# Deformable convolution and mixture of experts: images in pairs, positions without rows of their own

## The reference, cut to what matters

```python
xl = ln_c(x)                                  # normalised over channels
om = conv3x3(xl, w_off) + b_off               # 27 maps: 9 dy, 9 dx, 9 masks
ys, xs = y + kh - 1 + dy, x + kw - 1 + dx     # sampling places, per tap and pixel
sampled = bilinear(xl, ys, xs) * sigmoid(mask)   # zero outside the image
x = x + einsum('bckhw,ock->bohw', sampled, w_dcn)
t = tokens(x); z = ln_t(t)
w = softmax(top2(z @ Wg + bg))
t = t + sum_e w[e] * (gelu(z @ W1[e] + b1[e]) @ W2[e] + b2[e])
```

## Time and profile before

| | us |
|---|---|
| median of three runs | 90.9 |
| the profiled execution | 90.21 |
| its span, first to last instruction | 88.4 |
| PE busy | 80.9 (92%) |
| DVE busy | 64.5 (73%) |
| ACT busy | 46.9 (53%) |
| POOL busy | 20.6 (23%) |

### The profile page before, as it was taken

One profiled execution on the slowest core, in us unless ns is written; L12 is line 12 of the kernel. 1 busy time (PEld: TensorE's weight loads), 2 busy tenths in 40 slices (PEclk: granted clock), 3 DMA queues, 4 the chain that ended last, 5 costly groups with the idle time before them and its releaser, 6 DMA issues.

```text
span 88.4 us, 1853 instructions
## 1 busy us (share of the span) xinstructions
PE 80.9 (92%) x606; PEld 48.7 (55%) x606; DVE 64.5 (73%) x199; ACT 46.9 (53%) x95; POOL 20.6 (23%) x39
## 2 busy tenths in 40 slices
PE   3986799999999999969969999999999999999970
PEld 3974455499657968846646535734345332433540
DVE  5999989998999999999954998519667613213470
ACT  4110565787956843211410899814439986889000
POOL 7499820000003040005000002200309103200720
DMA  1520049340999997089999500000000000000012
GB/s 32 160 61 2 2 77 399 129 124 15 293 259 319 296 314 259 1 222 272 311 320 320 164 4 0 7 0 0 0 0 0 0 0 0 0 7 0 0 59 59
DMA packets 7192, 9.92 MB, mean 112 GB/s; under 512 B 1690, under 2 KB 3648, under 8 KB 7184
## 3 DMA queue, kind: packets, MB, share of 16 engines
q1 hardware_dynamic: 6848, 9.42, 35.9%
q0 software_dynamic: 192, 0.30, 1.0%
q10 hardware_dynamic: 144, 0.10, 0.3%
HBM read 8.95 MB, written 0.85 MB: 111 GB/s over the span
## 4 chain that ended last, share of the span: by engine, by line
PE 56%; DVE 19%; DMA 11%; issue 5%; SPq 3%; ACT 1%; POOL 1%; DVEq 0%
PE banks L937 17%; PE banks L948 15%; DMA hat_rows<-hlast 6%; DMA spread_hats<-hat_rows 6%; PE banks L861 5%; DVE front L589 4%; PE banks L875 4%; PE banks L830 3%; DVE xn L699 2%; PE banks L848 2%; SPq L335 2%; PE banks L928 1%; PE banks L886 1%; DVE spread_hats L600 1%; PE banks L919 1%
## 5 line engine op out<-in xcount | busy, mean ns | idle before, releaser
L511 ACT ACTIVATE front<-banks,b_col 128x512 f32<-128x512 f32 x32 | 19.8, 700 | 8.7 <-PE banks L937 5.4
L937 PE MATMUL banks<-x2s,w_sb 64*128 64x512 f32 x64 | 15.2, 608 | 0.0
L948 PE MATMUL banks<-front,w_sb 128*64 128x512 f32 (+1 forms) x72 | 14.7, 549 | 0.0
L770 DVE SCALAR_TENSOR_TENSOR spread_hats<-banks,b_col,spread 128x512 f32<-128x512 f32 (+1 forms) x9 | 6.1, 689 | 9.9 <-PE banks L948 7.3
L349 POOL TENSOR_TENSOR rs<-ve,power 128x2 f32<-128x2 f32 (+1 forms) x6 | 5.2, 868 | 28.7 <-DVE ve L639 27.5
L589 DVE TENSOR_TENSOR front<-hats 128x512 f32<-128x512 f32 (+1 forms) x20 | 11.5, 630 | 0.5 <-PE banks L861 0.3
L600 DVE TENSOR_TENSOR spread_hats<-spread_hats 128x1024 f32<-128x1024 f32 (+1 forms) x10 | 10.8, 1107 | 0.7 <-DMA spread_hats<-hat_rows 0.6
L483 ACT ACTIVATE smp<-banks 128x256 f32<-128x256 f32 x14 | 5.2, 389 | 9.5 <-PE banks L875 9.5
L875 PE MATMUL banks<-spread_hats,xn 128*64 128x256 f32 x72 | 9.0, 384 | 0.7 <-DVE spread_hats L600 0.7
L937 PEld LDWEIGHTS banks<-x2s,w_sb 64*128 64x128 f32 x64 | 5.7, 186 | 6.4 <-issue 2.5
L948 PEld LDWEIGHTS banks<-front,w_sb 128*64 128x64 f32 x72 | 4.9, 137 | 7.8 <-issue 6.2
(11 more groups left out here) (117 smaller groups left out, 102.0 us busy)
## 6 DMA issues: line engine op xcount, KB each, us to landing
spread_hats<-hat_rows SPq DMA_DIRECT2D x24, 256.0 KB, 5.0
w_sb<-in_w SPq DMA_DIRECT2D x2, 512.0 KB, 4.6
spread_hats<-hat_rows SPq DMA_DIRECT2D x6, 128.0 KB, 5.6
xc<-in_x_ch SPq DMA_DIRECT2D x1, 256.0 KB, 5.5
hat_rows<-hrow SPq DMA_DIRECT2D x2, 128.0 KB
hat_rows<-hrow POOLq DMA_DIRECT2D x2, 128.0 KB, 5.5
xt<-in_x_tok SPq DMA_DIRECT2D x1, 192.0 KB, 2.5
wdcn<-in_w_dcn SPq DMA_DIRECT2D x1, 160.0 KB, 2.9
```

Source lines behind the costliest of these rows:

```text
L511: act.activation(hid[:, m % H_RING, half, c, :], two_banks(f"H{h}.{j}.{c}")[:, half * 512:(half + 1) * 512], ACT.Gelu, bias=b1_col[:, col: ...
L770: dve.scalar_tensor_tensor(part(tmp[:, h, j, :]), part(bank(step_o)[:, :]), b2_col[:, j:j + 1], part(spread[:, h, j, :]), ALU.add, ALU.mul ...
L937: last = pe.matmul(two_banks(step)[:, half * 512:(half + 1) * 512], w1_sb[rows_, j, c * P:(c + 1) * P], x2s[rows_, 2 * h:2 * h + 2, :], st ...
L948: last = pe.matmul(part(bank(step)[O * half:O * half + O, :]), w2_sb[:, j + PAIRS * half, c, :], part(hid[:, (PAIRS * h + j) % H_RING, hal ...
```

## The change

- Convolution: xnT, xpl, xpu and conv take two images each. The 12 products of a pair go into four groups of 32 rows, two for each image, so that an image has two partial sums in place of four. Statistics are of four tiles and four tiles. xpu of the second pair is ACT's.
- Offsets: one om, one omT, one pos and one tanhm serve both DIRECT images, and one om serves both SPREAD images. The om of the DIRECT pair only copies; that of the SPREAD pair adds bias and pixel positions (pos_rows, made by POOL in place0) while copying, and is DVE's.
- Picking: R1.0 takes y and x of both images with 64 rows each, R1.1 the masks, R1.2 the ninth taps of both. The tap's own shift is the bias of ACT's abs (shift, made by POOL in shift0). The seven DMAs are gone.
- pick is made by two comparisons and two compare-and-add passes on DVE after four POOL iotas, ahead of the frames and the statistics.
- relu0 and relu1 go to ACT, the hat rows are split into y and x, xs1 and xs3 go to DVE, sel0 goes behind rstdt1.
- SP writes the hat rows of both SPREAD images before it issues the first read of them; before, POOL wrote those of image 3.
- All orders and banks are new.

```diff
+IMG_ROWS = 2 * OMG
+POS_ROW = OMG + OM
 PE_ORDER = (
-    "xnT0 early4 conv0 xnT2 xnT3 omT0 xnT1 conv2 conv3 conv1 R2.0 R2.1 R3.1 T0.0 T0.2 T0.3 R3.0 T0.1 T0.4 omT1 T0.5 T0.8 T0.7 "
-    "T0.6 M0.0 M0.4 M0.1 M0.3 M0.2 T1.0 T1.1 T1.3 T1.5 T1.2 T1.4 T1.7 T1.6 T1.8 M1.0 M1.3 M1.2 M1.4 M1.1 C0.0 C1.0 C0.1 C1.1 M2.2 "
-    "oT1 oT0 M2.0 M2.3 M2.1 M2.4 xT0 xT1 C2.0 M3.0 M3.1 C2.1 gate0 H0.2.0 H0.0.0 H0.1.1 H0.1.0 H0.0.1 H0.2.1 oT2 M3.3 M3.2 wdT0 "
...
+    "xnT0 early4 conv0 xnT1 omT0 conv1 R1.0 R1.2 R1.1 T0.5 T0.4 T0.2 T0.3 T0.0 T0.1 M0.2 M0.1 T0.8 M0.0 M0.4 T1.1 T1.0 T0.6 T0.7 "
+    "M1.0 M0.3 T1.3 T1.2 T1.4 T1.6 T1.5 T1.7 T1.8 C0.0 M1.2 M1.1 C0.1 M1.3 M1.4 oT0 C1.0 C1.1 M2.1 M2.0 oT1 M2.3 M2.2 xT0 M2.4 "
+    "C2.0 xT1 C2.1 M3.0 H0.2.0 gate0 H0.0.0 H0.2.1 oT2 H0.0.1 H0.1.1 H0.1.0 M3.1 M3.2 M3.3 O0.0 M3.4 C3.0 O0.2 C3.1 wdT0 xT2 "
...
 ACT_ORDER = (
-    "xpl0 om0 xpl2 xpl3 xpl1 tanhm0 abs0 om2 selr0 om3 ay2 al2 tm2 tl2 om1 E0.0 tm3 E0.3 ay3 E0.1 E0.2 tanhm1 E0.5 abs1 E0.7 E0.6 "
...
+    "xpl0 om0 xpu1 xpl1 tanhm0 abs0 relu0 abs1 relu1 ax2 tl2 al1 tm2 ay2 tl3 E0.5 E0.4 E0.2 E0.3 ay3 tm3 ax3 E0.1 E0.0 E0.8 se0.2 "
...
 DVE_ORDER = (
-    "stats0 stats1 xn0 base0 xpu0 xn2 xn3 xn1 xpu2 xpu3 pos0 dist0 xpu1 relu0 haty0 pr0.1.0 pr0.0.0 pr0.0.1 pr0.1.1 hr2.0 hr2.1 "
-    "hr2.2 pr0.2.0 pr0.2.1 pr0.4.0 pr0.4.1 pr0.3.0 pr0.3.1 pos1 dist1 E0.8 relu1 haty1 pr1.2.1 pr1.0.0 pr1.0.1 pr1.1.0 hr3.0 "
...
+    "stats0 stats1 xn0 xn1 xn2 xpu0 xn3 base0 pos0 dist0 dist1 om1 haty0 pr0.2.1 pr0.2.0 pr0.1.1 pr0.1.0 pr0.0.1 pr0.0.0 hy2 hx2 "
+    "hm2 hl1 pr0.4.1 pr0.4.0 hy3 hx3 haty1 hm3 pr1.0.0 pr1.0.1 pr0.3.1 pr0.3.0 pr1.2.0 pr1.3.1 se0.0 pr1.1.1 pr1.1.0 pr1.2.1 "
+    "pr1.3.0 pr1.4.1 pr1.4.0 E1.4 E1.2 pd2.0 pd2.1 se1.2 E1.8 se1.1 xr0 pd2.2 st0 xr1 pd2.3 lna0 st1 pd2.4 se2.1 lna1 pd3.0 xs1 "
+    "xr2 top0 pd3.1 idx0 pd3.2 pd3.3 pd3.4 se3.2 se3.3 st2 wd0 lna2 xr3 st3 lna3 xs3 ss0.1 tmp0.0 tmp0.2 top1 tmp0.3 tmp0.1 idx1 "
...
 POOL_ORDER = (
-    "rstd0 rows0 rstd1 sel0 dw3 rstdt0 rstdt1 rstdt2 rstdt3 ya0.1 ya0.2 ya0.3 ya1.1 ya1.2 "
+    "rstd0 rstd1 place0 shift0 rstdt0 rstdt1 sel0 rstdt2 rstdt3 ya0.1 ya0.2 ya0.3 ya1.1 ya1.2 "
...
         @block.sync
...
-            sp.wait_ge(ld_pos, 16 * 7)
+            for b in SPREAD:
+                write_rows(sp, b)
             for b in SPREAD:
                 i = SPREAD.index(b)
-                if i == 0:
-                    write_rows(sp, b)
                 sp.wait_ge(rows_written[b], 48)
...
             def make_constants():
...
-                dve.wait_ge(pool_index, 4)
-                dve.tensor_scalar(big[:, 2 * HW:], hat_of[:, :], pnum[:, 2:3], None,
-                                  ALU.is_equal).then_inc(pick_ready, 1)
+                dve.wait_ge(pool_index, 6)
+                parts = ((slice(0, 3 * P), row32), (slice(3 * P, 4 * P), row_img))
+                for part, number in parts:
+                    last = dve.tensor_scalar(pick[:, part], hat_of[:, part], number, None, ALU.is_equal)
+                chained(last)
+                for part, number in parts:
+                    last = dve.scalar_tensor_tensor(pick[:, part], place_of[:, part], number, pick[:, part], ALU.is_equal, ALU.add)
+                last.then_inc(pick_ready, 1)
...
                 elif kind == "conv":
...
-                    for i in range(2 * KS):
-                        kx, ky = divmod(i, KS)
-                        q = i % 4
+                    for t in range(2 * KS):
+                        kx, ky = divmod(t, KS)
+                        for i in range(2):
+                            q = 2 * i + t % 2
+                            last = pe.matmul(bank(step)[q * OMG:(q + 1) * OMG, 0:HW], woff[:, t, :],
+                                             xpad[:, 2 * b + i, ky:ky + H, 2 * kx:2 * kx + W], start=(t < 2), stop=(t >= 2 * KS - 2))
...
                 elif kind == "R":
...
+                        for c in ((0, 1) if n[1] == 0 else (2,)):
+                            for i in range(2):
+                                rows_ = slice(i * IMG_ROWS, (i + 1) * IMG_ROWS)
+                                first = i * 512 + c % 2 * HW
+                                last = pe.matmul(two_banks(step)[:, first:first + HW], pick[rows_, c * P:(c + 1) * P], om_sp[rows_, :],
+                                                 start=True, stop=True)
```

More of the change, by code:

```diff
@@ L247, in metaformer_kernel @@
[L247 to L251, removed]
+        pool_const, pool_index, pool_chain, place_chain, shift_chain, dve_chain, act_chain = (
+            sem(n) for n in ("pool_const", "pool_index", "pool_chain", "place_chain", "shift_chain", "dve_chain", "act_chain"))
@@ new lines, in metaformer_kernel @@
+        base_ready, fold_ready, omsum_ready, pick_ready, sel_ready, eight_ready, xpad_zeroed, boff_zeroed, bits_ready, pos_rows_ready = (
+            sem(n) for n in ("base_ready", "fold_ready", "omsum_ready", "pick_ready", "sel_ready", "eight_ready", "xpad_zeroed", "boff_zeroed",
+                             "bits_ready", "pos_rows_ready"))
+        var1, rstd1, xn1_ready, xn1T, xpad_low = (sem(n) for n in ("var1", "rstd1", "xn1_ready", "xn1T", "xpad_low"))
+        xpad_high = dict(ACT=sem("xpad_high_act"), DVE=sem("xpad_high_dve"))
@@ new lines, in metaformer_kernel @@
+        om_done, omT, pos_ready, tanh_done, abs_done = (sem(n) for n in ("om_done", "omT", "pos_ready", "tanh_done", "abs_done"))
+        relu_done = dict(ACT=sem("relu_act"), DVE=sem("relu_dve"))
+        dist_ready = dict(DVE=sem("dist_dve"), POOL=sem("dist_pool"))
+        haty_ready = dict(DVE=sem("haty_dve"), POOL=sem("haty_pool"))
+        at_ready = dict(DVE=sem("at_dve"), POOL=sem("at_pool"))
+        tap_made = dict(DVE=sem("tap_made_dve"), POOL=sem("tap_made_pool"))
+        hat_row = dict(DVE=sem("hat_row_dve"), POOL=sem("hat_row_pool"))
@@ new lines, in masked, with product @@
+        def masked(engine, b):
+            i = DIRECT.index(b)
+            engine.wait_ge(*saved(relu_done, f"relu{b}"))
+            engine.wait_ge(tanh_done, 1)
+            engine.scalar_tensor_tensor(hats[:, i, :, 0:TAPS, :], tanh_m[:, i, :, :].unsqueeze(3).broadcast_to([P, NT, TAPS, H]), 1.0,
+                                        hats[:, i, :, 0:TAPS, :], ALU.add, ALU.mult).then_inc(*one_more(haty_ready, f"haty{b}"))
+        def product(engine, b, q, j):
+            i = DIRECT.index(b)
+            u = CHUNKS * i + q
+            k0, m = chunk_taps(q)[0], len(chunk_taps(q))
+            engine.wait_ge(*saved(haty_ready, f"haty{b}"))
+            if u >= AT_RING:
+                before, chunk = divmod(u - AT_RING, CHUNKS)
+                engine.wait_ge(tap_T, upto(*(f"T{DIRECT[before]}.{k}" for k in chunk_taps(chunk))))
+            shape = [P, m, H, W]
+            engine.tensor_tensor(
+                at[:, u % AT_RING, j, 0:m, :].rearrange("p k (y x) -> p k y x", x=W),
+                hats[:, i, j, k0:k0 + m, :].unsqueeze(3).broadcast_to(shape),
+                hats[:, i, j, TAPS + k0:TAPS + k0 + m, :].unsqueeze(2).broadcast_to(shape),
+                ALU.mult).then_inc(*one_more(at_ready, f"pr{b}.{q}.{j}"))
@@ new lines, in make_places @@
+                    pool.iota(places[:, c, :].rearrange("p (y x) -> p y x", y=H), pattern=pattern, base=-(KS // 2), channel_multiplier=0,
+                              allow_small_or_imprecise_dtypes=True).then_inc(place_chain, 1)
+                pool.wait_ge(bits_ready, 1)
+                for c in range(2):
+                    pool.tensor_scalar(at_place[:, c:c + 1], pnum[:, 4:5], float(POS_ROW + c), None, ALU.is_equal).then_inc(place_chain, 1)
+                pool.wait_ge(place_chain, 4)
@@ L398, in _ @@
                     make_sel()
-                elif kind == "rows":
-                    make_rows()
+                elif kind == "place":
+                    make_places()
+                elif kind == "shift":
+                    make_shifts()
                 elif kind == "rstd":
-                    first, last = (0, NT) if n[0] == 0 else (NT, NB * NT)
+                    pair = FIRST_PAIR if n[0] == 0 else 1 - FIRST_PAIR
+                    tiles = slice(2 * NT * pair, 2 * NT * (pair + 1))
                     pool.wait_ge(pool_const, 3)
-                    rstd(var1, n[0] + 1, ve1[:, first:last], rs1[:, first:last], rstd1)
+                    rstd(var1, n[0] + 1, ve1[:, tiles], rs1[:, tiles], rstd1)
+                elif kind == "dist":
+                    distances(pool, n[0])
+                elif kind == "haty":
+                    masked(pool, n[0])
+                elif kind == "pr":
+                    product(pool, *n)
+                elif kind == "pd":
+                    spread_product(pool, *n)
+                elif kind == "hm":
+                    mask_rows(pool, n[0])
+                elif kind == "hl":
+                    last_rows(pool, n[0])
                 elif kind == "rstdt":
@@ L857, in _ @@
                     take_bank(step, saved(tap_saved, f"E{d}.{k}"))
[L858 removed]
```

(1 more changed line is left out.)

417 lines of the change are left out of this document (215 added, 202 removed), and 16 rows, old and new, of tables (ACT_ORDER, DVE_ORDER, PE_ORDER).

## The result

The changed kernel takes **95.48 us** (median of 4 executions, 95.09 to 95.91) where the kernel before takes 90.87 on the same chip (90.23 to 90.98). The ratio is 1.052, with a 95% interval of 1.046 to 1.059. It is slower by 4.6 us; forecast was 90.2, with a range up to 92.0.

A forecast was written before the change was run, and what follows sets the result against it. DVE bounds the front, PE close behind, and PE the experts. Experts from 45.9 plus PE's 39.1 end at 85.0, 0.9 before 85.88; 0.2 given back for handovers, the median 90.9 becomes 90.2, range 89.1 to 92.0.

The forecast's parts named there:

- what is put ahead of the statistics: Start: iotas, pick passes and frames on DVE delay the statistics 1.85 us, to 4.9; first product of hats at 16.8.
- the first rival: Start not won back: DVE bounds the front, first product at 18.2, end 91.6, or 92.0 with a DMA wait; chance 0.22.
- The order within the experts' part I cost at nothing: Experts' part: PE's sum stays the same; new waits could be 0.5 us less or 0.8 more.
- nothing is gained: Rival in the experts' part: O0.2, O1.1 and wdT1 closer to their inputs give back 0.7 us; 90.9; chance 0.12.
- the clock's fall: Rival at the start: PE's gap of 2.3 us drops its clock to 1.2 GHz; end 92.4; chance 0.08.
- the idle products' 4 us raise it just before: Argument against the clock falling at the start: idle products raise it, and each gap is broken after 2.3 us.
- The price, 2.7 us: Start at 1.2 GHz: conv0, omT0 and picking double, less 1.1 slack at om1; 2.7 us later, 2.2 reaching the end.
- the stretch behind the first product: DVE from first product of hats to pd3.0: 29.03 us becomes 26.8, so pd3.0 starts at 43.6.
- the 1.45 and 0.45 forecast: DVE behind the first product: pos1, dist1 and relu1 gone, 1.45 us; hat rows in fewer short passes, 0.45.
- The DMAs: Spread hats: SP's reads wait for image 3's writes, the last issued at 25.3; the 5.21 us write leaves the chain.
- the slack is thin: Reads before pd2.0: 0.5 us of slack where there were 7; beyond it, lateness of hm3 delays pd2.1 one for one.
- Picking: PE's front: R falls from some 4.2 us to about 1.9; two more tiling drains might cost 0.15 us each.

The follow-up runs named there:

- the late pick: Changed kernel with the four pick passes moved from ahead of the statistics to behind dist0: 92.37 us, ratio 1.018.
- 36 idle products: Changed kernel with 36 idle products on TensorE at the start instead of 18: 94.17 us, ratio 1.033.
- the kernel with the late pick: Changed kernel with pick behind dist0, GpSimd's sums waiting for wd1, selection held until pd3.0 is done: 91.16 us, ratio 0.991; run again, 91.05 us, ratio 1.000.
- the early selection: Changed kernel with GpSimd's sel0 right behind shift0, ahead of rstdt0 and rstdt1: 94.76 us, ratio 1.048.
- the control: The changed kernel once more, unedited, as yardstick of the first round: 95.27 us, ratio 1.046.
- O1.1 first: Changed kernel with O1.1 ahead of wdT1 in TensorE's order, as in the kernel before: 93.99 us, ratio 1.029.
- the sums that wait: Changed kernel with GpSimd's sums of head 0 waiting until wd1 is written: 93.45 us, ratio 1.031.
- GpSimd's writes: Changed kernel with GpSimd writing image 3's hat rows, so SyncE's reads don't queue behind them: 95.47 us, ratio 1.050.
- five edits: Changed kernel with pick behind dist0, 36 idle products, sums waiting for wd1, sel0 behind shift0 and O1.1 ahead of wdT1: 93.23 us, ratio 1.023.
- the repeated kernel: Changed kernel with pick behind dist0, sums waiting for wd1, selection held until pd3.0 is done, run in two rounds: 91.16 us, ratio 0.991; 91.05 us, ratio 1.000.

## Why the prediction was wrong, step by step

**Right: what is put ahead of the statistics.** They begin at 4.90, as forecast (1.83 late), a pair's convolution takes 1.50 at full clock, the first product comes at 16.90 when the clock holds. That a late start passes to the end one for one is shown by the late pick, 2.67 us at the first product and 2.56 at the experts; it holds as long as no DMA wait stands between, as with 36 idle products. The first product at 18.19 is also the figure of the first rival (18.2, end 91.6). That is luck: the statistics were on time and the clock made the difference, and the rival's end is still 3.9 short of 95.5.

**Failed: "The order within the experts' part I cost at nothing".** This was the largest miss, 2.4 us (41.5 for 39.1; the prediction allowed 0.8). The step reasoned with PE's sum and the slack of its inputs. What moved was where GpSimd's sums fall: wd1 had been made partly between them, now beside them. The rival *nothing is gained* named wdT1, but as standing too close to its weights, at 0.7 us; the weights themselves were late. With the sums held back and nothing else changed, PE's part from the first expert product to the last fold took 39.5 us, and again in both profiles of the kernel with the late pick (45.44 to 84.95; 46.93 to 86.45). So 2.0 of the 2.4 are the overlap; the other 0.4 lie within what the prediction allowed, and their cause stays open.

The Trainium skill, "SBUF — State Buffer", section "SBUF: two separate sides", describes a port pair shared by VectorE and GpSimd, which one of them holds for the length of an instruction. The traces agree: the small passes end with GpSimd's sums, 0.17 us becomes 0.79 to 1.12 and 0.19 becomes 1.14, and with the overlap gone they are short again. That the port is the mechanism no run shows apart from this timing.

**Failed: the chance given to the clock's fall (0.08).** In all six profiles with the long gap (2.3 to 2.8 us) PE was at the lower level in part of the start. In five it had risen and fell back, with a granted clock of 0.59 to 0.69 from 8.7 to 12.9 us; in the sixth, of the early selection, it had not risen before the convolution. The first product came at 17.7 to 18.2 for 16.90, so this cost 0.8 to 1.3 us there, and 1.1 at the end by the medians, 0.5 by the two profiles. The gap's place and length were forecast; "the idle products' 4 us raise it just before" was taken as protection, and isn't. The price, 2.7 us, was too high: the first convolution took 2.79 at most, not the 3.0 of a full doubling, and omT0 and the picking ran at none of the lower level. The Trainium skill, "TensorE: Matmul & The Clock Gate", part 1, says that the throttled state is the default; the granted clock of 0.59 behind the gap agrees.

**Mis-sized: the stretch behind the first product** (26.8 us forecast, 27.9 measured). The busy time of DVE over it, kernel before and then kernel after:

```profile
13.93:42.96 29.03, 28.21 (x248) 20.94 (x246) 27.93 (x63) 15.80 (x37) 3.36 (x5) 1.00 0.73 221
```

```profile
18.20:46.06 27.86, 27.54 (x249) 19.55 (x249) 26.03 (x59) 15.99 (x37) 2.33 (x4) 1.00 0.73 216
```

The work that goes was right: 27.93 less 26.03 is 1.90, the sum of the 1.45 and 0.45 forecast (that it agrees to the hundredth is chance). The idle time was taken to be 0.3 to 0.4 before and to go; by these rows it was 1.10 before and 1.83 after, 0.73 more instead of 0.35 less. DVE's waits over the stretch, longest first, kernel after:

```profile
DVE front L381 <- PE banks L944: 0.5, 1, 0.5
DVE hrow L796 <- ACT hrow L577: 0.3, 1, 0.3
DVE xn L822 <- POOL rs L416: 0.3, 1, 0.3
DVE hrow L796 <- ACT hrow L572: 0.2, 1, 0.2
DVE spread_hats L391 <- DMA spread_hats<-hat_rows: 0.2, 1, 0.2
```

Work moved off DVE leaves DVE waiting for who has it now: ACT's share of the hat rows, 0.5 in all, and the transposes, 0.5 (0.3 before). The change wins at most what is left.

**Missed: the selection beside pd3.0**, 0.46 us (1.68 against 1.22 with it moved). The change moves `sel0` in GpSimd's order and pd3.0 in time; the prediction followed neither to where they meet.

**The DMAs** were followed rightly in the order of their issues: reads began at 27.0 for 25.5, since the rest was late too, and the longest DMA wait was 0.2 us. That the slack is thin was right as well, and dearer than it looked: the same wait of DVE's spread products was 0.53 with O1.1 first, 0.77 with the sums that wait, 0.89 with GpSimd's writes and 1.41 with five edits, and there was none in the control. The changed kernel and the control are the same kernel, so its size varies from one execution to the next.

**Picking.** The three steps R1.0, R1.2 and R1.1 take 2.3 us with the clock up (16.64 to 18.97 with 36 idle products), for 1.9 forecast. R1.2 and R1.1 take 0.63 each from start to start; in the kernel before, picking products of 128 rows took 0.53 to 0.63. So the two changes of tiling mode show no cost clear of 0.1 us each.

## What to carry to other kernels

When an order on one engine is rewritten, look for what the *other* engines' long passes will lie beside: in the trace of before, a pass that takes several times its usual duration marks the collision and its price. Count idle products as cover for the clock only up to the moment they end. And remedies are to be tried together: here three that helped alone, or helped where they were aimed, cost as much elsewhere.

## What the runs showed of the hardware that had not been expected

- A DVE pass of 8 columns beside a GpSimd pass over 512 takes as long as GpSimd has left: 0.79 us for 0.17. Six products of 512 columns beside GpSimd's selection take 4.95 for 3.70, and one of 1024 takes 1.68 for 1.22 beside it.
- A granted clock of 1.00 says nothing ahead of TensorE's first quick product. In all fourteen profiles the stretch from 0 to 5.5 us reads 1.00, while the idle products go at the slow pace there (18 of them in 4.21 us). In the third round's profile of the repeated kernel, PE rose only during the first convolution: idle products took 0.24 us each and the convolution 2.15, and the record reads 1.00 over all of it:

```profile
5.50:8.70 3.20, 2.41 (x11) 2.04 (x11) 2.96 (x9) 0.60 (x1) 2.86 (x7) 1.00 0.52 124
8.70:12.90 4.20, 3.93 (x36) 2.16 (x34) 2.88 (x13) 1.22 (x3) 3.73 (x8) 1.00 0.58 221
```

  Where PE had risen and fell back, the record shows it (0.59). The duration of one known product tells more. Two of the four executions of the changed kernel list a mean clock of 1.000 and were no faster (95.91 and 95.64) than those with 0.982 (95.09 and 95.32). A late rise in place of a fall would look like that; no profile of these two shows it.
